# The beginning of a gated cross-attention kernel in another order: transfers, first weight turns, statistics, masks and scales

## The reference, cut to what matters

```
def layernorm(x): return (x - mean(x)) / sqrt(var(x) + 1e-5)

# x (16, 128, 128), ctx (16, 77, 128), 16 heads of 8
Q = layernorm(x) @ Wq.T + bq
K = ctx @ Wk.T + bk
V = ctx @ Wv.T + bv
# head h looks only at context rows h, h + 16, h + 32, h + 48: four keys
scores = einsum(Q, K_strided) / sqrt(8)
attn   = softmax(scores)
x = x + tanh(g_xattn[0]) * ((attn @ V_strided) @ Wo.T + bo)

x = x + tanh(g_ffn[0])   * transformer_block_with_8_experts(layernorm(x))
x = x + tanh(g_xattn[1]) * matching_attention(layernorm(x), ctx)
x = x + tanh(g_ffn[1])   * mixture_of_16_experts(layernorm(x))
```

## Time and profile before

| | us |
|---|---|
| runs, median of 3 | 509.56 (507.66 to 509.74) |
| the profiled execution, its own time | 510.12 |
| its span, first to last instruction | 508.4 |
| PE busy | 462.2 (91% of the span) |
| POOL busy | 319.2 (63%) |
| DVE busy | 356.5 (70%) |
| ACT busy | 286.8 (56%) |

### The profile page before, as it was taken

The page is one execution under the profiler, slowest core; times in us unless marked ns, Lnnn a source line. Parts: engine busy times, 40 slices in busy tenths (PEclk is TensorE's granted clock), DMA queues, the critical chain, the costliest instruction groups (busy, mean ns, idle before and its releaser), DMA issues.

```text
span 508.4 us, 10947 instructions
## 1 busy us (share of the span) xinstructions
PE 462.2 (91%) x3689; PEld 349.1 (69%) x3714; DVE 356.5 (70%) x918; ACT 286.8 (56%) x557; POOL 319.2 (63%) x525
## 2 busy tenths in 40 slices
PE   5879798999999599989998999899989999799895
PEld 5667465766676378767776878587767776677573
DVE  5356777899988547987764767667576757767763
ACT  2223386777785655556567456654765377446442
POOL 7875789898868556545764476355645583447453
PEclk9596799999999769999999999999999999999999
DMA  6420000030101000020000000000000000000000
GB/s 166 131 76 1 1 3 3 3 107 14 55 1 56 2 0 1 1 52 2 0 2 1 1 1 2 0 0 0 0 0 1 1 2 0 22 1 23 0 22 21
DMA packets 19337, 9.80 MB, mean 19 GB/s; under 512 B 6519, under 2 KB 18776, under 8 KB 19288
## 3 DMA queue, kind: packets, MB, share of 16 engines
q1 hardware_dynamic: 17848, 8.84, 6.3%
q10 hardware_dynamic: 1440, 0.33, 0.3%
HBM read 8.12 MB, written 1.05 MB: 18 GB/s over the span
## 4 chain that ended last, share of the span: by engine, by line
PE 59%; DVE 13%; issue 10%; POOL 9%; ACT 6%; DMA 2%; SPq 1%; POOLq 0%; ACTq 0%; DVEq 0%
PE PS L1821 11%; PE PS L1823 10%; PE PS L1822 10%; PE PS L1670 3%; PE PS L1676 3%; POOL HLO L614 2%; DVE work L1382 2%; PE PS L1665 2%; PE PS L1638 2%; PE PS L1710 2%; DVE work L1387 2%; DMA X<-in_x_dram 2%; PE PS L1876 1%; PE PS L1720 1%; PE PS L1653 1%
## 5 line engine op out<-in xcount | busy, mean ns | idle before, releaser
L614 POOL TENSOR_TENSOR HLO<-work,HHI 128x512 fp32r<-128x512 f32 x112 | 144.5, 1292 | 132.5 <-ACT HHI L862 126.2
L869 ACT ACTIVATE work<-PS 128x512 f32<-128x512 f32 x112 | 66.7, 596 | 92.4 <-PE PS L1823 88.6
L1382 DVE TENSOR_TENSOR work<-work,PS 128x512 f32<-128x512 f32 x104 | 71.1, 683 | 63.2 <-ACT work L869 30.6
L1387 DVE TENSOR_TENSOR work<-PS,work 128x512 f32<-128x512 f32 x112 | 77.2, 691 | 18.7 <-POOL HLO L614 10.0
L862 ACT ACTIVATE HHI<-work 128x512 fp32r<-128x512 f32 x111 | 69.7, 628 | 23.1 <-DVE work L1387 22.9
L1099 DVE TENSOR_REDUCE nmax<-PS 128x4 f32<-128x512 f32 x64 | 42.4, 683 | 7.9 <-PE PS L1638 7.5
L730 ACT ACTIVATE EX<-PS 128x512 f32<-128x512 f32 x64 | 34.9, 603 | 11.8 <-PE PS L1653 11.6
L1821 PE MATMUL PS<-HHI,W0H_down 128*128 128x512 f32 x72 | 35.0, 486 | 1.2 <-DVE work L1382 1.0
L1821 PE MATMUL PS<-H2H,W0H_gate 128*128 128x512 f32 (+1 forms) x72 | 32.5, 451 | 0.7 <-ACT work L869 0.7
L1821 PE MATMUL PS<-H2H,W0H_up 128*128 128x512 f32 (+1 forms) x72 | 29.7, 412 | 2.9 <-DVE work L1387 2.9
L1822 PE MATMUL PS<-H2L,W0H_up 128*128 128x512 f32 (+1 forms) x72 | 28.9, 401 | 0.0
(11 more groups left out here) (359 smaller groups left out, 1210.6 us busy)
## 6 DMA issues: line engine op xcount, KB each, us to landing
X<-in_x_dram SPq DMA_DIRECT2D x4, 256.0 KB, 6.6
raw<-in_L_ffn_e_gate_dram SPq DMA_DIRECT2D x1, 1024.0 KB, 5.3
raw<-in_L_ffn_e_up_dram SPq DMA_DIRECT2D x1, 1024.0 KB, 7.6
out_dram<-X SPq DMA_DIRECT2D x4, 256.0 KB, 2.3
ctx_nat<-in_ctx_dram SPq DMA_DIRECT2D x2, 308.0 KB
raw<-in_L_ffn_We_gate_dram SPq DMA_DIRECT2D x1, 512.0 KB, 3.8
raw<-in_L_ffn_We_up_dram SPq DMA_DIRECT2D x1, 512.0 KB, 3.9
raw<-in_L_ffn_We_down_dram SPq DMA_DIRECT2D x1, 512.0 KB, 4.1
```

Source lines behind the costliest of these rows:

```text
L614: pool.tensor_tensor(HLO[t][:], HH[k % 2][:], HHI[t][:].bitcast(F32), ALU.subtract).then_inc(m_sem["lo"], 1)
L869: act.activation(SG[c % 2][:], PS[:, c % 2, :], ACT.Silu).then_inc(S["silu"], 1)
L1382: dve.tensor_tensor(SG[c % 2][:], SG[c % 2][:], PS[:, 4, :], ALU.mult).then_inc(S["scaled"], 1)
L1387: dve.tensor_tensor(HH[c % 2][:], PS[:, 2 + c % 2, :], SG[c % 2][:], ALU.mult).then_inc(S["hid"], 1)
```

## The change

It reorders the beginning and replaces one computation.

- Transfers: Wk and Wv go to the head of SP's queue with a semaphore of their own; context half 0 stays behind the tokens of group 0, and tokens 1 come ahead of context half 1. ACT's queue issues the three biases, then Wq and Wo. Gates and bo move from ACT's queue to SP's, behind the tokens of group 3.
- PE: 4 filler turns and the turns of Wk and Wv alone; context 0 and 1; 4 filler turns; keys_values(0); the turn of Wo; keys_values(1); context 2 and 3; 5 filler turns; then fold_keys(0) and on as before. ACT copies Wo's turned block by itself, and its Tanh of the gates comes behind folded_keys(0), waiting for gates and bo.
- Statistics: `bn_aggr` behind `bn_stats` gives mean and variance on VectorE, in place of arithmetic on the raw statistics on VectorE (group 0) and GpSimd (the others).
- VectorE's order: statistics 0, scales 0, masks 0, statistics 1, masks 1, statistics 2 and 3, row maximum 0.
- GpSimd's order: BQ, normalised 0, scales 1, normalised 1, clearing of KS, tgbo, bias 0, scales 2 and 3, bias 1, and on as before.

```diff
@@ SP
+            for i, n in enumerate(("Wk", "Wv")):
+                sp.dma_start(w_nat[:, i, :], a["L0_xattn_" + n]).then_inc(wkv_in, 16)
             tokens(0)
             context(0)
+            tokens(1)
             context(1)
-            for g in range(1, G):
+            for g in range(2, G):
                 tokens(g)
+            sp.dma_start(gates[:, 0:2], row(a["g_xattn"], P)).then_inc(gates_in, 16)
+            sp.dma_start(gates[:, 2:4], row(a["g_ffn"], P)).then_inc(gates_in, 16)
+            sp.dma_start(bo_r[:], row(a["L0_xattn_bo"], P)).then_inc(gates_in, 16)
@@ GpSimd, first_scales and order
                 pool.wait_ge(dve_c, hi)
-                moments(at, n)
-                step(pool.tensor_scalar(p_a[:, 0:n], var[:, at], LN_EPS, None, ALU.add))
+                pool.tensor_scalar(mean[:, at], amoments[:, at, 0], -1.0, None, ALU.mult)
+                step(pool.tensor_scalar(p_a[:, 0:n], amoments[:, at, 1], LN_EPS, None, ALU.add))
                 inverse_root(rstd[:, at], p_a[:, 0:n], p_b[:, 0:n])
                 step(pool.tensor_tensor(nmr[:, at], mean[:, at], rstd[:, at], ALU.mult))
...
-            normalised_group(0)
             pool.wait_ge(bias_in, 16 * 3)
             pool.tensor_copy(BQ[:], bq_c[:].broadcast_to([P, P])).then_inc(a_sem["bq"], 1)
+            normalised_group(0)
+            first_scales(1, 2)
+            normalised_group(1)
             for u in range(NKS):
                 step(pool.memset(KS[u][:].bitcast(F32), 0.0))
                 step(pool.memset(KS[u][:, :, 48:50], 1.0))
             pool.sem_inc(consts, 1)
-            first_scales(1, G)
-            normalised_group(1)
             pool.wait_ge(tg_ready, 1)
-            pool.wait_ge(bo_in, 16)
             step(pool.tensor_scalar(tgbo[:], bo_r[:], tg[:, 0:1], None, ALU.mult))
             bias_group(0)
+            first_scales(2, G)
             bias_group(1)
@@ ACT
-            for i, n in enumerate(("Wk", "Wv", "Wo", "Wq")):
-                act.dma_start(w_nat[:, i, :], a["L0_xattn_" + n]).then_inc(wa_in, 16)
             for n, dst in (("bk", bk_c), ("bv", bv_c), ("bq", bq_c)):
                 act.dma_start(dst[:], col(a["L0_xattn_" + n])).then_inc(bias_in, 16)
-            act.dma_start(gates[:, 0:2], row(a["g_xattn"], P)).then_inc(gates_in, 16)
-            act.dma_start(gates[:, 2:4], row(a["g_ffn"], P)).then_inc(gates_in, 16)
-            act.dma_start(bo_r[:], row(a["L0_xattn_bo"], P)).then_inc(bo_in, 16)
+            for i, n in ((3, "Wq"), (2, "Wo")):
+                act.dma_start(w_nat[:, i, :], a["L0_xattn_" + n]).then_inc(wa_in, 16)
...
             folded_keys(0)
+            act.wait_ge(gates_in, 16 * 3)
+            act.activation(tg[:], gates[:], ACT.Tanh).then_inc(tg_ready, 1)
             turned_group(0)
@@ VectorE
                         ins = dve.bn_stats(stats[:, g * GB + j, :], X[:, g * GB + j, :])
+                    lnc(ins)
+                    for j in range(GB):
+                        ins = dve.bn_aggr(amoments[:, g * GB + j, :], stats[:, g * GB + j, :])
                     ins.then_inc(dve_c, 1)
...
             first_stats(0, 1)
-            first_scales(0, 1)
-            first_stats(1, G)
+            first_scales()
             masked_keys_values(0)
+            first_stats(1, 2)
             masked_keys_values(1)
+            first_stats(2, G)
             less_row_maximum(0)
@@ PE
-            keep_going(18, PS[:, 7, 0:P])
-            pe.wait_ge(wa_in, 16 * 4)
-            for i in range(3):
+            keep_going(4, PS[:, 7, 0:P])
+            pe.wait_ge(wkv_in, 16 * 2)
+            for i in range(2):
                 ins = pe.transpose(PS[:, 0, i * D:(i + 1) * D], w_nat[:, i, :], identf[:])
             ins.then_inc(pre_ps, 1)
...
+            def turn_output_weights():
+                pe.wait_ge(wa_in, 16 * 2)
+                pe.wait_ge(pre_sb, 1)
+                pe.transpose(PS[:, 0, 2 * D:3 * D], w_nat[:, 2, :], identf[:]).then_inc(pre_ps, 1)
+
+            turn_context(0)
+            turn_context(1)
+            keep_going(4, PS[:, 7, 0:P])
...
             keys_values(0)
-            keep_going(6, PS[:, 7, 0:P])
+            turn_output_weights()
+            keys_values(1)
+            turn_context(2)
+            turn_context(3)
+            keep_going(5, PS[:, 7, 0:P])
             fold_keys(0)
-            keys_values(1)
             fold_values(0)
```

More of the change, by code:

```diff
@@ L674, in _ @@
             act.wait_ge(pre_ps, 1)
-            act.activation(w_t[:].rearrange("p a b -> p (a b)"), PS[:, 0, 0:3 * D], ACT.Copy).then_inc(pre_sb, 1)
+            act.activation(w_t[:, 0:2, :].rearrange("p a b -> p (a b)"), PS[:, 0, 0:2 * D], ACT.Copy).then_inc(pre_sb, 1)
             for k in range(4):
                 if k == 2:
-                    act.wait_ge(gates_in, 16 * 2)
-                    act.activation(tg[:], gates[:], ACT.Tanh).then_inc(tg_ready, 1)
-                act.wait_ge(pre_ps, 2 + k)
+                    act.wait_ge(pre_ps, 4)
+                    act.activation(w_t[:, 2, :], PS[:, 0, 2 * D:3 * D], ACT.Copy).then_inc(pre_sb, 1)
+                act.wait_ge(pre_ps, 2 + k + k // 2)
                 act.activation(ctx_t[:, 4 * k:4 * k + 4, :], PS[:, 1 + k, 0:4 * TC].rearrange("p (a b) -> p a b", a=4),
@@ L996, in rsqrt @@
                     chain(dve.scalar_tensor_tensor(out=dst, in0=tb, scalar=1.5, in1=dst, op0=ALU.add, op1=ALU.mult))
-            def moments(st=stats, chain=lnc, lo=0, n=B):
-                ta, tb, tc, mn, vr = (some(t, lo, n) for t in (t_a, t_b, t_c, mean, var))
-                st = st[:, lo:lo + n, :]
-                chain(dve.tensor_tensor(ta, st[:, :, 1], st[:, :, 4], ALU.add))
-                chain(dve.tensor_scalar(mn, ta, 0.5, None, ALU.mult))
-                chain(dve.tensor_tensor(tb, st[:, :, 1], st[:, :, 4], ALU.subtract))
-                chain(dve.scalar_tensor_tensor(out=tc, in0=tb, scalar=0.25, in1=tb, op0=ALU.mult, op1=ALU.mult))
-                chain(dve.tensor_tensor(ta, st[:, :, 2], st[:, :, 5], ALU.add))
-                chain(dve.scalar_tensor_tensor(out=vr, in0=ta, scalar=1.0 / D, in1=tc, op0=ALU.mult, op1=ALU.add))
-            def scales(rs=rstd, nm=nmr, chain=lnc, lo=0, n=B):
-                rs, nm = some(rs, lo, n), some(nm, lo, n)
-                rsqrt(rs, some(var, lo, n), LN_EPS, chain, lo, n)
-                chain(dve.scalar_tensor_tensor(out=nm, in0=some(mean, lo, n), scalar=-1.0, in1=rs, op0=ALU.mult, op1=ALU.mult))
             for s in at_one["dve"]:
@@ L1021, in first_stats, with first_scales @@
                         ins = dve.bn_stats(stats[:, g * GB + j, :], X[:, g * GB + j, :])
+                    lnc(ins)
+                    for j in range(GB):
+                        ins = dve.bn_aggr(amoments[:, g * GB + j, :], stats[:, g * GB + j, :])
                     ins.then_inc(dve_c, 1)
-            def first_scales(lo, hi):
-                dve.wait_ge(dve_c, hi)
-                moments(lo=lo * GB, n=(hi - lo) * GB)
-                scales(lo=lo * GB, n=(hi - lo) * GB)
+            def first_scales():
+                dve.wait_ge(dve_c, 1)
+                rsqrt(rstd[:, 0:GB], amoments[:, 0:GB, 1], LN_EPS, lnc, 0, GB)
+                lnc(dve.scalar_tensor_tensor(out=nmr[:, 0:GB], in0=amoments[:, 0:GB, 0], scalar=-1.0, in1=rstd[:, 0:GB],
+                                             op0=ALU.mult, op1=ALU.mult))
                 dve.sem_inc(a_sem["ln"], 1)
@@ L1522, in _, with turn_context @@
             pe.wait_ge(consts, 1)
-            keep_going(18, PS[:, 7, 0:P])
-            pe.wait_ge(wa_in, 16 * 4)
-            for i in range(3):
+            keep_going(4, PS[:, 7, 0:P])
+            pe.wait_ge(wkv_in, 16 * 2)
+            for i in range(2):
                 ins = pe.transpose(PS[:, 0, i * D:(i + 1) * D], w_nat[:, i, :], identf[:])
             ins.then_inc(pre_ps, 1)
-            for k in range(4):
+            def turn_context(k):
                 pe.wait_ge(ctx_in[k // 2], 16)
@@ L1543, in fold_keys @@
                 pe.wait_ge(a_sem["kv_sb"], g + 1)
+                if g == 0:
+                    pe.wait_ge(pre_sb, 4)
                 if g >= 1:
```

18 lines of the change are left out of this document (4 added, 14 removed).

## The result

The kernel after takes 509.69 us (median of 20 executions, 507.79 to 511.9), the kernel before on the same chip 507.1 (20 executions, 502.95 to 509.74). The ratio is 1.0058 with a 95% interval of 1.0040 to 1.0077: 0.6% slower, where 0.5% faster was forecast. The 20 executions of before also show that the 509.56 of the first three, and the profiled execution's 510.12, lay near the top of what this kernel does. The profiled execution after has 510.26 (span 508.3), and its first turn of the next stage starts at 40.84, in the profiled before at 40.25. The point followed by the prediction had been put at 37.5.

A forecast was written before the change was run, and what follows sets the result against it. It took the wait chain ending in TensorE's `attend(1)`, with half-clock stretches, as the bound. The next stage's first turn moves from 40.25 to 37.5, so 510.12 - 2.75 = 507.4 us; forecast 505.5 to 508, range 503.8 to 510.5.

The forecast's parts named there:

- the new stall of TensorE for the normalised group 2: After `attend(0)`, TensorE was to wait from 26.1 to 28.0 us for GpSimd's normalised group 2.
- no idle time ahead of `scales_of_group(0)`: On GpSimd, idle 2.72 us before, now none or under 0.3 us; `scales_of_group(0)` starts at 32.5 instead of 33.7.
- GpSimd's queue late next: GpSimd delivers Z at 37.4, after TensorE ends `attend(1)` at 33.4 (high clock) or 36.7 (low).
- ScalarE's Tanh: Ahead of the turned group's copy, due at 15.1, it waits for bo, landing by 15.4; cost nothing, at most 0.3 us.
- The power for 4 elements: GpSimd's power step in the scales of group 1 alone, estimated at 1.04 us from the slope of 2.30 and 1.67.
- it waits for the statistics of group 1 until 12.15 (+1.0): GpSimd, done with normalised group 0 at 11.15, waits until 12.15 for VectorE's statistics of group 1: +1.0 us.
- Transfers: Wk and Wv head SP's queue; first tokens land at 4.9 (4.05 to 5.2), context half 0 at 6.1, late end 7.0.
- The masks: VectorE's masks of group 0 follow `keys_values(0)`: context at 6.1, masks 9.75 to 10.75 at the low clock.
- The statistics behind the masks: VectorE's statistics and aggregates of group 1, after the masks of group 0 end at 10.75, done at 12.1.
- Rival 2: Low-clock stretch begins after the stall at 26 to 28, over before 42: gain 4.8 us, 504.8; chance 0.14.
- Rival 3: TensorE at the low clock from its start until 25.4, with less filler: gain 0.5 us, 509.0; chance 0.12.
- rival 4: TensorE's low clock continues until 31 from too little work: 2.3 us slower than now, 511.8; chance 0.12.

The follow-up runs named there:

- scales together: Kernel after with GpSimd's order of before: KS cleared behind normalised group 0, scales of groups 1 to 3 in one piece, both biases together; 512.33 us, ratio 1.0087.

## Why the prediction was wrong

**What held.** The mechanism was that of the forecast: the new stall of TensorE for the normalised group 2, no idle time ahead of `scales_of_group(0)`, GpSimd's queue late next, the first turn waiting for Z. ScalarE's Tanh cost nothing (16.21, no wait for gates or bo). The power for 4 elements took 1.04, as estimated from the slope. GpSimd from the scales of group 1 to `scales_of_group(0)` took 20.8 us (14.98 to 35.76); predicted were 20.35 (12.15 to 32.5). The scales apart were 3.18 + 3.98 against 6.18, so +1.0 and not +0.7.

**The step that failed** is the start of that queue: "it waits for the statistics of group 1 until 12.15 (+1.0)". It waited until 14.98, for 2.58 us. This +2.83 is nearly all of the 3.3 by which the first turn missed 37.5, and it has three terms:

- The landings in "Transfers". The tokens were put at 4.9, between 4.05 and 5.2, and landed at 6.74 (5.57 to 6.74 over the nine profiles with SP's new order; 4.05 to 4.64 over the seven with the old). The context was put at 6.1, with 7.0 as the late end; its turns started at 8.82 (7.61 to 8.82 over the same nine; 6.04 and 6.61 with the old transfers in the kernel after). The sum took the full rate of the earlier trace rows for the first microseconds; that row was of a stretch in which other transfers went. The sum also counted only the bytes that stand ahead: up to 8.8 us the core had moved 1.32 MB (150 GB/s from the start of the span), of which Wk, Wv, the first tokens and the first half of the context are 0.69 MB, so that transfers issued later had shared the wires. The three small issues that now head ScalarE's queue got no term, as they move 1.5 KB. Which of these made the landing late is not settled. The prediction itself had named tokens landing after 5.5 as a sign of being wrong.
- The masks. Context at 6.1 to masks at 9.75 are 3.65 us; measured, 8.82 to 12.82, are 4.0. Here the low clock was taken, rightly, but the eight context turns were put at 1.05 and took 1.29; its own row, 16 of them in 1.23 at the high clock, gives 1.23 for eight at half the speed. The high-clock case was put too small as well: 0.5 us earlier, where the kernel with 18 filler turns started GpSimd's queue at 12.80, 1.6 to 2.2 earlier.
- The statistics behind the masks: 12.82 to 14.98 are 2.16 against 2.4 predicted. This term was right, so the transfers carry the miss: 2.7 of the 2.83.

The old transfers did not repair it, though (1.78 us of wait left, 0.6 of the gain lost on the way to the masks). With the order given to VectorE, either set of transfers makes GpSimd wait. What repairs it is work for the gap.

**The base was the second failure.** The prediction set its gain off from 40.25 and noted 0.56 us to the median shown. That execution was 3.0 us above the median of 20, and had its low stretch (15.2 to 25.4) where the other profile of before has none; its GpSimd had "1.6 us to spare behind it and 2.7 ahead of it", while the other had none ahead. Against 38.49 even the predicted 37.5 would have been a gain of 1.0 us, and the kernel would have been expected at about 506. Rival 2 was in part what happened to the clock (high 14.1 to 31, then a fall behind the stall), but in the other execution of before that stretch was at the high clock already, so there was nothing to give back. How often before runs the one way or the other, two profiles can't say.

**The rivals.** Rival 3 and 4 asked for a low clock until 25 or later and didn't happen: it rose at 14.0. The 0.12 for "slower" had only rival 4 in it. What was missing is the slower case of the forecast's own mechanism: GpSimd's queue, with a start 2 us later than worked out, ends behind TensorE's program. From the prediction's own numbers the point at which it decides could be had: Z at 37.4 + x against a first turn of 40.25, so x = 2.85 to lose against the profile, and about 1 against the other execution.

**The clock.** The 4 filler turns took 1.09 us (0.27 each) under a page of the profile that gives 1.00, as in the earlier trace rows, and `keys_values(0)` ran at 0.85 for two matmuls until 12.7 (0.44 at the high clock). The Trainium skill (TensorE: Matmul & The Clock Gate, Part 1) says that the throttled state is the default and that activity releases it. The traces agree at the start of the changed kernel (with 18 turns the clock rises at 8.9, with 4 between 11.3 and 14.0 over the seven profiles with SP's new order), less so in the second profile of before (18 turns, and the 16 context turns from 9.56 still took 2.26 us, as at the low clock), and they don't show what should release it at 22 to 46 us of the kernel with the masks first, where TensorE was 90% busy.

## What to carry to other kernels

Before work is moved ahead on a busy engine, follow the queue that feeds it: an engine won time here only to wait for a supplier whose own start had been put behind the moved work, and the masks moved ahead alone, without the supplier's part, lost as well (ratio 1.0076). Where an in-order queue gets a gap, put in it what is needed later (the clearing), and put behind its urgent output what can wait (the biases of later groups). It took this and the new order together to make the kernel that beats both (503.06 us): the late biases in the old order gained nothing that was measured. And take the base from several executions: the start of the next stage in a second profile of the same kernel differed by 1.8 us, two thirds of the gain that was being forecast.

## What the runs showed of the hardware

- **Small transfers at the head of a queue.** From 2 to 3 us the core moved 404 packets in after and 383 in before, but at 92 GB/s against 195: in after 227 of them were under 512 bytes, in before 2. ScalarE's queue has 204 of these, and it carries the biases then, one element of 4 bytes for each partition. The Trainium skill (DMA: Bandwidth & Descriptors, Queues, rings and completion order) says that each DMA engine takes turns between queue rows, a packet at a time. The trace agrees, with 204 packets of ScalarE's queue beside 200 of SP's queue in that microsecond. With the biases behind two weights the slow microseconds came later (133 and 113 GB/s from 3 to 5 us) and the context's turns began at 8.72, so that the packets are the cause of the late landing is not shown.
- **Around the end of a long wait the clock falls, for very different times.** With 4.07 us of waiting TensorE ran at 1.2 GHz for 24 us (masks first; busy 21.32 of 23.80), with 2.76 us for 13.5 (after; busy 12.30), with 3.21 us for 6.9 (scales together; busy 5.41). With 3.45 us it was 17.1 us with the biases last and 3.4 with 18 filler turns: the lengths don't follow the waits. The clock also fell behind shorter waits (1.47 us in the kernel before, at 35.7).
- **Low-clock time costs this kernel less than half.** The fit gives 0.28 us for each microsecond at 1.2 GHz in place of the 0.5 that the prediction took. That other engines set the pace in part of this time is my reading of it, not tested.
- **ScalarE's issues hold its first activation.** The table load (1.28 us) started at 4.32 with five issues on its queue and at 6.96 with ten (6.82 in the kernel before, also ten).
